# Attention with exact top-k thresholds and a gated feed-forward layer: two PSUM banks for the transposed scores, one for all other products, and a block search one slot earlier

## What is computed

```
U = min(L, int(5 * log(L)))                       # 31
scores = einsum('bhqd,bhkd->bhqk', Q, K) / sqrt(D)
thresh = top_k(scores, U)[..., -1:]
scores = where(scores < thresh, -inf, scores)
context = softmax(scores) @ V
x = layernorm(x + context @ Wo.T + bo)
h = silu(x @ wg.T) * (x @ wu.T)
out = layernorm(x + h @ wd.T)
```

## Time and profile before

| | |
|---|---|
| median of 3 executions | 3084.57 us |
| the profiled execution's own time | 3082.59 us |
| its span | 3080.8 us |
| TensorE matmul busy | 2733.1 us (89%) |
| VectorE busy | 2502.0 us (81%) |
| ScalarE busy | 2496.6 us (81%) |
| GpSimd busy | 2401.5 us (78%) |
| TensorE's mean granted clock | 0.954 |

### The profile page before, as it was taken

One profiled execution on the slowest core, in us unless ns is written; L12 is line 12 of the kernel. 1 busy time (PEld: TensorE's weight loads), 2 busy tenths in 40 slices (PEclk: granted clock), 3 DMA queues, 4 the chain that ended last, 5 costly groups with the idle time before them and its releaser, 6 DMA issues.

```text
span 3080.8 us, 81076 instructions
## 1 busy us (share of the span) xinstructions
PE 2733.1 (89%) x21030; PEld 1498.6 (49%) x21375; DVE 2502.0 (81%) x12298; ACT 2496.6 (81%) x5894; POOL 2401.5 (78%) x1677
## 2 busy tenths in 40 slices
PE   5988989899998998889989998988989998998986
PEld 2444545455454454544545454444545545454554
DVE  4888888888888878888888888878888888888851
ACT  4888888888889877788888888878878887898852
POOL 1888887788788877788788787877878787788881
PEclk7899999999999999999999999999999999999987
DMA  2201011110111101011010111102111010111000
GB/s 85 48 20 44 22 50 29 28 44 24 38 27 40 38 22 42 19 43 36 25 45 25 37 29 36 39 20 47 25 35 37 25 44 26 36 30 32 20 16 7
DMA packets 91143, 102.64 MB, mean 33 GB/s; under 512 B 34513, under 2 KB 52946, under 8 KB 90578
## 3 DMA queue, kind: packets, MB, share of 16 engines
q1 hardware_dynamic: 88544, 93.73, 12.7%
q10 hardware_dynamic: 2034, 2.76, 0.3%
HBM read 20.86 MB, written 8.39 MB: 9 GB/s over the span
## 4 chain that ended last, share of the span: by engine, by line
PE 51%; ACT 19%; issue 14%; DVE 12%; SPq 1%; POOL 1%; ACTq 1%; DVEq 1%; DMA 0%; POOLq 0%
ACT above L479 8%; PE bench L681 6%; PE Y_ps L617 6%; PE ST_ps L628 6%; PE bench L687 6%; PE ST_ps L631 6%; PE ctxT_ps L645 5%; ACT junk L469 5%; DVE cand L877 5%; PE bench L558 4%; PE Y_ps L615 4%; ACT PT L487 3%; PE Y_ps L614 3%; PE bench L674 2%; PE bench L589 2%
## 5 line engine op out<-in xcount | busy, mean ns | idle before, releaser
L1109 POOL TENSOR_SCALAR mask<-S,thr,mb 128x512 bf16<-128x512 f32 x1024 | 2114.0, 2077 | 42.9 <-POOL mb L1103 34.6
L877 DVE MAX8 cand<-Y_ps 128x8 f32<-128x128 f32 x4096 | 1075.5, 283 | 6.7 <-issue 6.7
L870 DVE TENSOR_SCALAR_CACHE_REDUCE S<-S_ps,na 128x512 f32<-128x512 f32 x1024 | 758.1, 740 | 298.7 <-PE S_ps L604 240.7
L469 ACT ACTIVATE junk<-S,at_zero,slope 128x512 bf16<-128x512 f32 x1024 | 824.8, 805 | 96.5 <-DVE S L870 96.5
L479 ACT ACTIVATE above<-S,s,steep 128x512 bf16<-128x512 f32 x1024 | 825.1, 806 | 0.6
L487 ACT ACTIVATE PT<-ST_ps 128x512 f32<-128x512 f32 x1024 | 596.9, 583 | 224.2 <-PE ST_ps L631 222.9
L628 PE MATMUL ST_ps<-QS,KS 64*128 64x512 f32 x1024 | 457.3, 447 | 122.2 <-ACT PT L487 117.0
L604 PE MATMUL S_ps<-KS,QS 64*128 64x512 f32 x1024 | 523.5, 512 | 4.2 <-DVE S L870 2.8
L617 PE MATMUL Y_ps<-KS,QS 64*128 64x512 f32 x1024 | 523.1, 511 | 1.0 <-issue 0.7
L615 PE MATMUL Y_ps<-above,nbig 128*128 128x512 bf16 x1020 | 399.0, 391 | 74.9 <-DVE cand L877 49.6
L631 PE MATMUL ST_ps<-nbig,mask 128*128 128x128 bf16 x4096 | 417.9, 226 | 0.0
(11 more groups left out here) (125 smaller groups left out, 3681.5 us busy)
## 6 DMA issues: line engine op xcount, KB each, us to landing
QS<-Qhi SPq DMA_DIRECT2D x512, 32.0 KB, 2.0
KS<-Khi SPq DMA_DIRECT2D x512, 32.0 KB, 2.0
KS<-Klo SPq DMA_DIRECT2D x512, 32.0 KB, 2.0
QS<-Qlo SPq DMA_DIRECT2D x512, 32.0 KB, 2.0
xTs<-in_xT SPq DMA_DIRECT2D x17, 512.0 KB, 3.8
xs<-in_x SPq DMA_DIRECT2D x16, 512.0 KB, 3.9
out<-xs SPq DMA_DIRECT2D x16, 512.0 KB, 2.9
hT<-in_wgT ACTq DMA_DIRECT2D x1, 768.0 KB
```

The lines of the kernel that those rows point to most:

```text
L469: nc.scalar.activation(junk[:, :], S[:, score_place(j)[0], :], ACT.Tanh, bias=at_zero[:, :], scale=slope[:, hb, col:col + 1], accum_out=s0 ...
L870: nc.vector.tensor_scalar(S[:, at, :], S_ps[n % 2][:, :], na[:, hb, col:col + 1], None, ALU.add, op1=ALU.max, accum_out=rmax[:, n % RING:n ...
L877: mx = nc.vector.max(cand[:, j % CANDS, i, :], Y_ps[j % 2][:, i * BW:(i + 1) * BW])
L1109: nc.gpsimd.tensor_scalar(mask[:, h % MASKS, t, :], S[:, score_place(j)[0], :], thr[:, r:r + 1], mb[:, r:r + 1], ALU.is_lt, op1=ALU.add).t ...
```

## The change

There is one bench bank, with one `ready` and one `taken`, and the bank set free goes to the transposed scores, which now alternate between two. A product on the bench waits until the product before it, of whatever kind, is taken. No slot has two products any more: gate and up get slots of their own (gate 42, 44, 46, 49, 51, 53; up 43, 45, 47, 50, 52, 54), and q, keys, the Gram matrix, the quadratic form, the sums and the transposed context move by one to four slots. BLOCK is 4 instead of 5 (and SORT 5 instead of 6). On VectorE the residuals and the low part of x1 move ahead of the copy of the scores; row statistics stay behind it. `th` has two places, used in turn; tanh of part i waits for GpSimd's product of part i-2, and the copy to `ups` for that of part i-1. The small tiles of the output bias lie in `th` and `ups`, and ScalarE waits once, before batch 1, for the DMAs that read them.

```diff
-BLOCK = 5
-SORT = 6
+BLOCK = 4
+SORT = 5
...
-HALF_USES = {4: "v", 11: "q", 12: "k", 13: "keys", 14: "gram", 15: "quad", 17: "sums",
-             26: "v", 33: "q", 34: "k", 35: "keys", 36: "gram", 37: "quad", 56: "sums"}
+HALF_USES = {4: "v", 10: "q", 12: "k", 14: "keys", 17: "gram", 19: "quad", 21: "sums",
+             26: "v", 33: "q", 34: "k", 35: "keys", 36: "gram", 37: "quad", 55: "sums"}
 VALUES_AT = (4, 26)
-CTX_T, OUT_PROJ, X1_T = (27, 28), (30, 31), (38, 39)
-FFN_SLOTS = {43: 0, 45: 1, 47: 2, 50: 3, 52: 4, 54: 5}
+CTX_T, OUT_PROJ, X1_T = (28, 29), (30, 31), (38, 39)
+GATE_SLOTS = {42: 0, 44: 1, 46: 2, 49: 3, 51: 4, 53: 5}
+UP_SLOTS = {43: 0, 45: 1, 47: 2, 50: 3, 52: 4, 54: 5}
 DOWN_SLOTS = {58: 0, 59: 1, 60: 2, 61: 3}
...
-        th = sb("th", [P, L])
+        th = sb("th", [P, 2, L])
         ups = sb("ups", [P, L])
+
+        brow = th[0:1, 0, 0:DM]
+        bparts = [ups[0:1, i * (DM // 2):(i + 1) * (DM // 2)].bitcast(BF16) for i in range(3)]
...
-        ST_ps = ps("ST_ps", [P, L])
+        ST_ps = [ps(f"ST_ps{i}", [P, L]) for i in range(2)]
         ctxT_ps = ps("ctxT_ps", [P, L])
-        bench = [ps(f"bench{i}", [P, L]) for i in range(2)]
+        bench = ps("bench", [P, L])
...
-        ready = [sem(f"ready{i}") for i in range(2)]
-        taken = [sem(f"taken{i}") for i in range(2)]
+        ready = sem("ready")
+        taken = sem("taken")
...
                         if what == "gate":
-                            act.wait_ge(ready[k], use + 1)
+                            act.wait_ge(ready, use + 1)
+                            if part > 1:
+                                act.wait_ge(h_done, (b - 1) * NF + part - 1)
+                            nc.scalar.activation(th[:, part % 2, :], bench[:, :], ACT.Tanh, scale=0.5 * DEQ).then_inc(th_done, 1)
+                        if what == "up":
+                            act.wait_ge(ready, use + 1)
                             if part:
                                 act.wait_ge(h_done, (b - 1) * NF + part)
...
-                if not (first and n == TURNED):
-                    pe.wait_ge(exp_done, T - TURNED)
-                nc.tensor.matmul(ST_ps[:, :], KS[rows, r, kt * P:(kt + 1) * P], QS[rows, r, :], start=True, stop=False,
+                ST = ST_ps[j % 2]
+                if not (first and n < TURNED + 2):
+                    pe.wait_ge(exp_done, T - TURNED - 1)
+                nc.tensor.matmul(ST[:, :], KS[rows, r, kt * P:(kt + 1) * P], QS[rows, r, :], start=True, stop=False,
                                  tile_position=(rows.start, 0))
...
             def on_bench(b, n, first, rest):
                 for what, part in uses_of(n, first, rest):
-                    k, use = place(b, n, what, part, first, rest)
-                    pe.wait_ge(taken[k], use)
+                    use = place(b, n, what, part, first, rest)
+                    pe.wait_ge(taken, use)
...
                     evacuate(T, n, b, first)
                     for what, part in uses:
...
-                        if what == "out_proj":
-                            if part == 0:
-                                dve.wait_ge(x_loaded, b * 16)
-                            residual((2 * part, 2 * part + 1), (k, use))
...
                         if what == "down":
-                            residual((part,), (k, use))
-                            row_statistics(b, 1, (part,), (k, use))
+                            row_statistics(b, 1, (part,), use)
```

More of the change, by code:

```diff
@@ L128, with count @@
 TURN_OF, ACT_TURN_OF = 5, 7
[L130 to L138, removed]
+def count(first, rest, upto=(TILES, None)):
+    have = 0
     for n in range(TILES):
@@ L586, in project_values @@
                 for t in range(NT):
[L587 removed]
+                    o = bench[:, t * w:(t + 1) * w]
                     for c in range(C):
@@ L829, in moments, with head_gram, quadratic_terms @@
-            def moments(part, at):
+                dve.nop(nofuse=True).then_inc(taken, 1)
+            def head_gram(use):
+                dve.wait_ge(ready, use + 1)
+                nc.vector.tensor_tensor(gram[:, :], bench[:, 0:P], blk[:, :], ALU.mult).then_inc(taken, 1)
+            def quadratic_terms(use):
+                dve.wait_ge(ready, use + 1)
+                nc.vector.tensor_tensor(quad[:, :], bench[:, :], hi[0][:, :].bitcast(F32),
+                                        ALU.mult).then_inc(taken, 1)
@@ L842, in moments @@
+                    dve.wait_ge(taken, use + 1)
                     dve.nop(nofuse=True)
@@ new lines, in slots @@
+                        if what == "out_proj":
+                            if part == 0:
+                                dve.wait_ge(x_loaded, b * 16)
+                            residual((2 * part, 2 * part + 1), use)
+                        if what == "x1_t":
+                            dve.wait_ge(x1T_copied, b * 2 - 1 + part)
+                            to = [x1T[j][:, :, part * 2 * P:(part + 1) * 2 * P].rearrange("p c (n t) -> p n c t", n=2)
+                                  for j in range(2)]
+                            nc.vector.tensor_tensor(to[1], bench[:, :].rearrange("p (n c t) -> p n c t", n=2, c=C),
+                                                    to[0].bitcast(F32), ALU.subtract).then_inc(taken, 1)
@@ L1031, in slots @@
+                        if what == "down":
+                            residual((part,), use)
                         if what == "turn":
-                            normalise((n - 1 - GROUP) // 16 % NG, b * NG + n // 16 - 1, (k, use))
+                            normalise((n - 1 - GROUP) // 16 % NG, b * NG + n // 16 - 1, use)
                     for part in range(3):
@@ L1139, in slots @@
                     for what, part in uses_of(n - 1, first, rest) if n else []:
[L1140 to L1142 removed]
                         if what == "up":
[L1144 to L1146 removed]
+                            use = place(b, n - 1, "up", part, first, rest)
+                            pool.wait_ge(taken, use + 1)
+                            nc.gpsimd.tensor_tensor(hT[:, part, :], th[:, part % 2, :], ups[:, :], ALU.mult).then_inc(h_done, 1)
                     if not rest and HALF_USES.get(n - 4) == "sums":
```

318 lines of the change are left out of this document (131 added, 187 removed).

## The result

| | before | after |
|---|---|---|
| median | 3085.69 us (4 runs, 3081.59 to 3086.96) | 3474.57 us (4 runs, 3470.37 to 3490.13) |
| span of the profiled execution | 3080.8 us | 3475.4 us |
| mean granted clock of TensorE | 0.954 | 0.925 |

The ratio is 1.127, with a 95% interval of 1.1235 to 1.1309: the changed kernel is slower by 389 us, where 70 were forecast.

The account below looks back on a forecast made before the run. The prediction took TensorE, busy 2733.1 of 3080.8 us, as the bound. Bench waits of 252 us less gains of 182 gave +70 on 3082.59, 3153, put at 3155 us as a median; range 3040 to 3245 us.

Parts of the forecast that it names:

- The forecast's case: Whole kernel: new bench waits outweigh the old waits removed, slower at 3155 us; chance 0.52.
- gains: Steady part: waits for the exponential (106 us) and part of the search waits (76 us) go, 182 us together.
- No change: Rival for the whole kernel: bench waits and gains cancel, 182 us against 182, 3085 us; chance 0.10.
- Faster: Rival: only odd slots wait at the bench, 153 us against 220 us gained, 3018 us; chance 0.20.
- Bench waits: Steady part: TensorE waits for VectorE to free the one bank, 17.4 us a batch, 252 us counted.
- The start of the chain: Each slot: VectorE's search starts 0.35 us after the score product, its operation of length x frees the bench at 1.43 + x.
- Late slots of VectorE: Even-slot bench waits: 0.67 us in slot 34, 0.63 in 42 and 58, 0.55 in 50 and 54.
- Slots 0 to 25: Stretch with three engines almost full: nearly all search waits lie here; slot 10's 9 us bench wait counted at nothing.
- Clock: Steady part: granted clock 0.97 left as it is, nothing added to the sum.
- third case: Rival, much slower by the clock: time at 1.2 GHz doubles from 6 to 12%, 83 us more, 3238 us; chance 0.18.
- The ends: First batch and stretch behind last scores: gate and up pairs cost 9 us more, others offset; sum nothing, -10 to +10.
- What would show it: Signs in the changed profile: exponential waits under 20 us, search waits under 40, bench waits 200 or more.

Follow-up runs that it names:

- the run with earlier picks: VectorE's three pick and threshold steps moved one slot earlier, against the changed kernel: 3481.21 us, ratio 1.1276.
- the kernel with bench operations last: Changed kernel with VectorE's bench operations (all but the row sums of the first estimates) also behind its copy of the scores: 3888.93 us, ratio 1.2596.
- the fastest one: Changed kernel with bench operations ahead of search, picks one slot earlier, and a free score bank lent to some last-batch products: 3058.66 us, ratio 0.9912.
- 3085: Changed kernel with VectorE's bench operations ahead of sort and search in each slot: 3084.95 us, ratio 1.0014.
- 3113: Changed kernel with the search five slots behind again (BLOCK = 5, SORT = 6): 3113.04 us, ratio 1.0104.
- 3172: Changed kernel with the search five slots behind and one bank of transposed scores instead of two: 3172.2 us, ratio 1.0279.
- 3177 us: Changed kernel with bench operations ahead of the search and the search five slots behind: 3176.52 us, ratio 1.0289.

## Why the prediction was right in its mechanism and wrong in its size

The forecast's case came: one bank, freed by VectorE behind a search without a head start, and the product of the next slot waiting for it. Its gains were near, 200 us of old waits gone against 182. "No change" and "Faster" fell. The time lies 320 us over the forecast and 230 over its range. By the terms of its sum:

- **Bench waits, 252 forecast, 491 measured.** This is the step that failed, in three parts.
  - *The start of the chain.* "[T]he masked scores are the product just before, some 0.22 us earlier, so the search starts 0.35 us after the score product." It starts at 0.60 (1161.17 to 1161.77). The two products, one over each half of the array's 128 rows, start together: at 1161.17 in the timeline above, and in the trace of before at 1047.93, where the earlier trace rows shows only the second of them. The line missing there is

```profile
1047.93 0.50 PE L617 MATMUL Y_ps<-KS,QS 64*128 64x512 f32 x1
```

  Both readers then start about 0.6 us behind: 0.57 for the copy of scores, 0.60 for the search. The Trainium skill, "TensorEngine Tiling (Array Packing)", section "Key Properties", says that different tiles of the array can execute matmuls in parallel. The trace agrees, with the two starts above. The bank of slot 45 was free at 2.39 (1161.17 to 1163.56), forecast 2.11. In slots 26 to 61, at the places where VectorE has nothing else to do first, this made 16.7 us a batch of 13.8: 43 us.
  - *Late slots of VectorE.* The chain was costed as if VectorE came to each slot with nothing but the search ahead. To slots 34, 42, 50, 54 and 58 it comes late from those before. In slot 58 of batch 5 it is still at the variance (L820) and the copy of scores, the context's reader starts 3.06 us after the score product, where 1.4 were assumed, and the down product waits 2.31:

```profile
1201.49 0.50 PE L596 MATMUL S_ps<-KS,QS 64*128 64x512 f32 x1
1201.69 0.18 DVE L820 TENSOR_SCALAR sd<-sd 128x32 int32<-128x32 int32 x1
...
1202.09 0.75 DVE L840 TENSOR_SCALAR_CACHE_REDUCE S<-S_ps,na 128x512 f32<-128x512 f32 x1 [0.22 <-PE S_ps L596]
...
1203.49 0.29 DVE L847 MAX8 cand<-Y_ps 128x8 f32<-128x128 f32 x1
...
1204.55 0.24 DVE L939 RECIPROCAL rden<-bench 128x16 f32<-128x16 f32 x1
1204.82 0.42 DVE L941 TENSOR_TENSOR ctxs<-bench,rden 128x256 f32<-128x256 f32 x1
...
1205.44 2.19 PE L680 MATMUL bench<-wd,hT 128*128 128x256 f32 x5 [2.31 <-DVEq L945]
```

  These five places cost 8.3 us a batch against 3.0: 80 us. That they are late is read from the trace; no run took that work away, and the run with earlier picks shows that such waits partly move elsewhere.
  - *Slots 0 to 25.* "Slot 10 lies where TensorE isn't short of time; its 0.63 x 15 = 9 us I count at nothing". Bench waits there are 7.7 us a batch, 115 us in all, the largest ahead of the flags in slot 24 (2.42 us in batch 5), which were in no list. The flags' product has 78.2 of the 115 us, at slots 0, 8, 16 and 24; it waits for the flags, not for the bank, and the forecast had no term for that. Beside these waits the removed search waits bought nothing: the stretch takes 69.6 us on the mean of batches 2 to 14, where it took 68.4.
- **Clock, 0 forecast, +73 us.** The granted clock of the steady part fell from 0.97 to 0.95. Summed over the traces, TensorE was busy at 1.2 GHz for 122 us of it before and for 302 in the changed kernel. The same work at 2.4 GHz would take half, so the rise of 180 us costs some 90 by this estimate, enough for the 73. The forecast kept this for its third case (+83), and gave it 0.18. It was a part of the outcome beside the waits rather than another case.
- **The ends, 0 forecast, +34.** The chain of a pair was right link by link, but its products were priced at 1.13 us to their reader from a stretch in which the bench never ran dry. Alone between waits they run at the lower of the two clock levels (granted clock 0.50, 1.2 GHz), 2.08 and 2.07 us. Twice some 0.95 more on 4.29 gives the 6.2 us measured. That stretch of the changed kernel:

```profile
3417.50:3450.00 32.50, 21.79 (x43) 11.95 (x41) 3.43 (x5) 6.16 (x11) 6.38 (x5) 0.50 0.00 0
```

  Some 19 us come from that against 9 forecast: from the first gate product to the sixth it is 31.2 us where it was 15.8, and the last pair adds its part. (Before, only three of the five distances were 2.82 us; the first two were 3.55 and 3.73.) The version that lends it a bank of the scores gave 29 back. The first batch is 9 us longer, which no run followed up.
- **Sum.** 70, and 239 for the bench, 73 for the clock, 34 for the ends, less 18 for gains larger than taken: 398, where 394.6 were measured. The difference is the 4 us that TensorE was idle at the bench before, which the 491 hold and the forecast's 252 did not.

"What would show it" named VectorE idle before the search (682.6 us), old waits under 20 and 40 us (7.9 and 12.1) and bench waits of 200 us and more. All were seen. Not seen in their size were slot 45 at 3.6 us (3.96) and gate waits of 0.55 us in slots 50 and 54, which are 1.38 and 1.25 on the mean of 15 batches. "TensorE's busy time stays near 2730 us if the clock stays" was the line that gave the second cost away: 2819.9.

## What to carry to other kernels

Two edits that each remove slack from the same loop must be costed as one: here a bank and a slot of lag cost 46 and 52 us apart and 408 together, so follow the loop once round (product, reader, what the reader's engine does first, release, next product) and compare its length with the slot's, in every slot in which the reader's engine has extra work, not in the average one. When a buffer becomes single, put the instruction that frees it ahead of work that waits for the same engine; that order alone was worth 390 us here, and the reverse order was right as soon as the search was needed sooner. And price a product inside a wait-bound chain from a row of such a chain, not from a stretch where TensorE runs without pause.

## What the runs showed that was not expected

**The clock does not follow the idle time alone.** Two stretches of a batch have the same share of TensorE idle time in the changed kernel (19% in slots 26 to 41 and in slots 42 to 63), on the mean of batches 2 to 14, yet different clocks. Batch 6 of the changed kernel, a batch with more idle time than the mean (27 and 24%), slots 26 to 41 and 42 to 63:

```profile
1299.45:1364.27 64.82, 47.54 (x346) 24.97 (x351) 44.92 (x205) 41.03 (x98) 37.16 (x29) 0.88 0.14 33
1364.27:1452.10 87.83, 66.90 (x479) 38.16 (x487) 58.70 (x273) 53.94 (x125) 57.68 (x40) 0.94 0.07 15
```

and of the kernel with bench operations last:

```profile
1456.61:1531.42 74.81, 52.75 (x345) 27.91 (x350) 46.17 (x209) 42.88 (x103) 37.27 (x30) 0.82 0.14 33
1531.42:1636.49 105.07, 76.01 (x481) 43.75 (x488) 58.29 (x269) 53.27 (x123) 57.42 (x39) 0.85 0.05 11
```

Over batches 2 to 14 the mean clock of slots 26 to 41 is 0.98, 0.92 and 0.78 (before, changed, bench last), that of slots 42 to 63 0.99, 0.97 and 0.88, that of slots 0 to 25 0.95, 0.93 and 0.94. The first stretch has many short products between its waits, the second four-part products of 1.2 us; whether that is the cause no run tells.

**A chain of single products drops the clock to one half.** Behind the last scores the same products ran at 0.50 on one bank (the row of 3417.50 to 3450.00 us) and at 0.95 to 0.99 with two, in the kernel before and in the fastest one (12.07 us busy of 15.50):

```profile
3016.50:3032.00 15.50, 12.07 (x44) 7.75 (x42) 3.69 (x6) 6.34 (x11) 6.49 (x5) 0.95 0.00 0
```

**Neither the number of banks nor the sum of idle time sets it in the steady part.** With one bench bank it is 0.97 to 0.98 in the four kernels with 221 to 322 us of idle time (3085, 3113, 3172 and 3177 us), 0.95 in the changed kernel with 547 and 0.87 with 741; with two bench banks and the short lag it is 0.95 at 205 and 237 us. (The traces hold 19,672 to 19,677 matmul records for the kernel before, the changed one, the one of 3177 us and the one with 741 us, and 20,002 to 20,004 for the others; idle time looks somewhat longer where records are missing.) The Trainium skill, "TensorE: Matmul & The Clock Gate", section "A second HAM failure mode: psum-queue depth-cycling", says that short idle times between groups of matmuls, from cycling through PSUM banks, make the clock swing and cost throughput. The trace agrees in part: waits of 1 to 2 us came with 73 and 302 us of busy time more than before, but one bank whose reader is early costs little in clock: 0.97 in the steady part with bench operations first and with the search five slots behind, as before the change.
